# Softmax sums of a graph layer: one VectorE instruction for the leaky score, odd blocks finished on ScalarE and GpSimd

## What is computed

```python
Wh = h @ W.T
s1 = Wh @ a1
s2 = Wh @ a2
e = jax.nn.leaky_relu(s1[rows] + s2[cols], negative_slope=NEG_SLOPE)   # 0.2
e = e - jnp.max(e)
exp_e = jnp.exp(e)
sum_exp = jax.ops.segment_sum(exp_e, rows, num_segments=N)
alpha = exp_e / (sum_exp[rows] + EPS)
h_prime = jax.ops.segment_sum(alpha[:, None] * Wh[cols], rows, num_segments=N)
```

## Time and profile before

| | us |
|---|---|
| median of 3 runs | 8971.87 (8968.87 to 8975.18) |
| profiled execution | 8960.56 |
| its span in the trace | 8958.4 |
| `soft_sums`, passes 0, 1, 2 (first to last VectorE instruction of the blocks) | 236.65, 223.35, 224.63 |
| between pass 0's last and pass 1's first | 9.9 |

### The profile page before, as it was taken

The page is one execution under the profiler, slowest core; times in us unless marked ns, Lnnn a source line. Parts: engine busy times, 40 slices in busy tenths (PEclk is TensorE's granted clock), DMA queues, the critical chain, the costliest instruction groups (busy, mean ns, idle before and its releaser), DMA issues. The chain is left out here.

```text
span 8958.4 us, 195643 instructions
## 1 busy us (share of the span) xinstructions
PE 7343.9 (82%) x51013; PEld 5653.7 (63%) x51014; DVE 6057.0 (68%) x12581; ACT 5103.3 (57%) x9231; POOL 3338.0 (37%) x3274
## 2 busy tenths in 40 slices
PE   5999999888869999999877777777787877777774
PEld 3656666577758778788756556555565655555554
DVE  7988988899952222222456666666666777777777
ACT  3666666688846666666544444444456655555553
POOL 0000000000000000000067777777756777777776
PEclk8999999999989999999978888888889998988897
DMA  3333333366633333333222222222226666666665
GB/s 112 138 134 136 137 137 138 144 227 225 224 101 123 124 125 125 123 124 125 69 70 55 54 55 54 54 54 54 54 54 192 202 195 195 196 194 197 196 194 157
DMA packets 629188, 1179.08 MB, mean 132 GB/s; under 512 B 215307, under 2 KB 289340, under 8 KB 609685
## 3 DMA queue, kind: packets, MB, share of 16 engines
q1 hardware_dynamic: 499834, 860.28, 29.7%
q0 software_dynamic: 129280, 317.93, 12.7%
HBM read 901.19 MB, written 276.57 MB: 131 GB/s over the span
## 5 line engine op out<-in xcount | busy, mean ns | idle before, releaser
L2269 POOL DMA_INDIRECT att_kv_rows<-kv_dram,att_stage x1616 | 1646.1, 1019 | 520.4 <-issue 482.4
L2024 POOL DMA_INDIRECT conv_rows<-y_dram,conv_stage x1616 | 1626.9, 1007 | 501.1 <-issue 478.8
L1013 DVE SCALAR_TENSOR_TENSOR mean_rest<-mean_counts,mean_high 128x896 f16<-128x896 f32 x343 | 377.5, 1101 | 1110.5 <-ACT mean_high L974 1110.5
L694 PE MATMUL conv_part<-conv_msgs,conv_hot 128*128 128x256 f32 x3232 | 945.3, 446 | 0.0
L694 PE MATMUL att_part<-att_msgs,att_hot 128*128 128x128 f32 x3232 | 517.4, 309 | 474.1 <-DVE att_msgs L2413 434.7
L2002 ACT ACTIVATE conv_hid<-conv_hid_ps 100x512 f32<-100x512 f32 x408 | 221.0, 594 | 1179.1 <-PE conv_hid_ps L2033 1179.1
L694 PEld LDWEIGHTS conv_part<-conv_msgs,conv_hot 128*128 128x128 f32 x3232 | 710.7, 231 | 107.0
L694 PEld LDWEIGHTS att_part<-att_msgs,att_hot 128*128 128x128 f32 x3232 | 436.9, 210 | 535.7 <-issue 338.7
L1067 PE MATMUL mean_sum_ps<-wh,mean_turned 128*128 128x129 f32 x4802 | 696.2, 285 | 51.6 <-ACT mean_turned L982 51.3
L234 PE MATMUL count_ps<-count_cols,count_rows 128*128 128x392 bf16 x3920 | 730.1, 331 | 8.5 <-DVE count_cols L200 8.5
L1958 POOL MEMSET acc<- 128x6656 f32 x1 | 5.6, 5644 | 1902.8 <-POOLq L1882 1902.8
(11 more groups left out here) (279 smaller groups left out, 16592.8 us busy)
## 6 DMA issues: line engine op xcount, KB each, us to landing
c_dram<-count_counts SPq DMA_DIRECT2D x392, 392.0 KB, 2.3
mean_counts<-c_dram SPq DMA_DIRECT2D x343, 448.0 KB, 4.0
att_w_rows<-w_dram SPq DMA_DIRECT2D x404, 256.0 KB
soft_counts<-c_dram SPq DMA_DIRECT2D x98, 1024.0 KB, 4.9
w_dram<-mlp_w SPq DMA_DIRECT2D x294, 256.0 KB, 2.7
mlp_feats<-in_feats SPq DMA_DIRECT2D x295, 192.0 KB, 2.7
soft_counts<-c_dram SPq DMA_DIRECT2D x49, 1088.0 KB, 5.0
att_lanes<-lo_dram SPq DMA_DIRECT2D x404, 128.0 KB
```

The source lines that it names most:

```text
L694: ins = nc.tensor.matmul(part, c.hot[:, s, t, :], rows[:, t, :], start=half == 0 and t == 0, stop=half == 1 and t == T - 1)
L1013: nc.vector.scalar_tensor_tensor(rest[:, m], counts[:, m], 0.25, high[:, m], ALU.mult, ALU.subtract).then_inc(rest_done, 1)
L2024: pool.indirect_dma_start(rows[:, s, t, :], None, y_dram, bass.IndirectOffsetOnAxis(ap=stage[:, s, t:t + 1], axis=0)).then_inc(gathered[s] ...
L2269: pool.indirect_dma_start(kv_rows[:, s, t, :], None, kv_dram, bass.IndirectOffsetOnAxis(ap=stage[:, s, t:t + 1], axis=0)).then_inc(gathere ...
```

## The change

VectorE now makes the leaky score itself, in one scalar_tensor_tensor: max(s1 + 0.8 s2, 0.2 s1), which is the leaky score less 0.2 s2 (`bend`). `s1_low` (0.2 s1, made once for each pass) lies in the last part of `acc`; 0.8 s2 and the rest of the shift are columns of `shift`. Even blocks go on with one exponential on ScalarE and min and counts on VectorE (`weigh`). For odd blocks ScalarE takes a relu of the negated exponent, which is the min with 1, and then the exponential, and GpSimd multiplies with the counts. `weights` has six buffers instead of two, all steps work in place in them, and `exps` is gone. The loop bodies hold twelve blocks (`rounds` is 4), and VectorE and ScalarE work ahead: two blocks for even ones, five for odd ones.

```diff
-    rounds = (NW - 1) // 6
+    rounds = (NW - 1) // 12
+    evens, odds = (NW + 1) // 2, NW // 2
...
+        s1_low = acc[:, firsts[2]:NW + 1].rearrange("p n f -> p (n f)")
-        exps = sb("exps", [P, 2, 2, widest])
-        weights = sb("weights", [P, 2, widest])
-        shift = sb("shift", [P, 2, NW])
+        weights = sb("weights", [P, 6, widest])
+        shift = sb("shift", [P, 3, NW])
...
+                    elif r % 2:
+                        sp.wait_ge(weighed_even, even(p, i, r - 3))
+                    else:
+                        sp.wait_ge(weighed_odd, odd(p, i, r - 3))
...
+            @block.gpsimd
+            def _(pool):
+                for p in range(3):
+                    with pool.Fori(0, rounds) as i:
+                        for r in range(1, 12, 2):
+                            pool.wait_ge(exp_odd, odd(p, i, r))
+                            wait_counts(pool, p, i, r)
+                            nc.gpsimd.tensor_tensor(slot(p, r), slot(p, r), counts_of(p, r), ALU.mult).then_inc(weighed_odd, 1)
...
-                    dve.wait_ge(exp_done, n + 1)
-
-                    dve.wait_ge(summed, n + 1)
-                    nc.vector.tensor_tensor(here, exps[:, b, 0, 0:wide], exps[:, b, 1, 0:wide], ALU.max).then_inc(larger, 1)
-                    dve.wait_ge(counts_in[s], 16 * count)
-                    dve.wait_ge(larger, 2 + n + 1)
-                    nc.vector.scalar_tensor_tensor(here, here, 1.0, counts[:, s, 0:wide], ALU.min, ALU.mult).then_inc(weighed, 1)
+                    dve.wait_ge(summed, NW * p + w + 1)
+                    nc.vector.scalar_tensor_tensor(slot(p, r), s1_row[:, 0:wide], shift[:, 2, bass.ds(w, 1)], s1_low[:, 0:wide],
+                                                   ALU.add, ALU.max).then_inc(bent_odd if r % 2 else bent_even, 1)
+
+                def weigh(p, i, r):
+                    dve.wait_ge(exp_even, even(p, i, r))
+                    wait_counts(dve, p, i, r)
+                    nc.vector.scalar_tensor_tensor(slot(p, r), slot(p, r), 1.0, counts_of(p, r), ALU.min, ALU.mult).then_inc(weighed_even, 1)
...
+                    dve.wait_ge(s1_in[p], 16)
+                    nc.vector.tensor_scalar(s1_low[:, 0:wide], s1_row[:, 0:wide], 0.2, None, ALU.mult).then_inc(low_done, 1)
+                    dve.wait_ge(low_done, p + 1)
...
+                def body(p, i, last):
+                    for r in range(0, 12, 2):
+                        bend(p, i, r + 2)
+                        weigh(p, i, r)
+                        if not last or r < 8:
+                            bend(p, i, r + 5)
...
-                    nc.scalar.activation(exps[:, b, 0, 0:wide], row, ACT.Exp, bias=shift[:, 0, at])
-                    nc.scalar.activation(exps[:, b, 1, 0:wide], row, ACT.Exp, scale=0.2, bias=shift[:, 1, at]).then_inc(exp_done, 1)
+                    nc.scalar.activation(slot(p, r), slot(p, r), ACT.Exp, bias=shift[:, 0, bass.ds(12 * i + r, 1)]).then_inc(exp_even, 1)
+
+                def exp_of_odd(p, i, r):
+
+                    act.wait_ge(bent_odd, odd(p, i, r))
+                    nc.scalar.activation(slot(p, r), slot(p, r), ACT.Relu, scale=-1.0, bias=shift[:, 1, bass.ds(12 * i + r, 1)]).then_inc(turned, 1)
+                    act.wait_ge(turned, odd(p, i, r))
+                    nc.scalar.activation(slot(p, r), slot(p, r), ACT.Exp, scale=-1.0).then_inc(exp_odd, 1)
```

More of the change, by code:

```diff
@@ L428, in place, with slot, even, odd @@
             return ps[:, b // 3, b % 3 * (D + 1):(b % 3 + 1) * (D + 1)]
+        def slot(p, r):
+            return weights[:, (p + r) % 6, 0:widths[p] * P]
+        def even(p, i, r):
+            return evens * p + 6 * i + r // 2 + 1
+        def odd(p, i, r):
+            return odds * p + 6 * i + r // 2 + 1
         with nc.Block() as block:
@@ L442, in _ @@
                     if p > 0:
[L444 removed]
+                        sp.wait_ge(bent_even, evens * p)
+                        sp.wait_ge(bent_odd, odds * p)
                     sp.dma_start(s1_row[:, 0:wide], s1_dram[firsts[p] * P:firsts[p] * P + wide].partition_broadcast(P)).then_inc(s1_in[p], 16)
[L446 to L448 removed]
@@ L449, in _, with wait_counts, counts_of @@
-                    load(p, NW - 1, NW * p + NW - 1, p % 3)
+                    for r in range(12):
+                        load(p, 0, r, True)
+                    with sp.Fori(1, rounds) as i:
+                        for r in range(12):
+                            load(p, i, r, False)
+                    load(p, rounds, 0, False)
+            def wait_counts(eng, p, i, r):
+                eng.wait_ge(counts_in[(p + r) % 3], 16 * (4 * i + (NW * p + r) // 3 + 1))
+            def counts_of(p, r):
+                return counts[:, (p + r) % 3, 0:widths[p] * P]
@@ L477, in take @@
                     dve.wait_ge(taken, 2 * (p + 1))
[L479 to L482, removed]
-                for p in range(3):
[L484 to L491, removed]
+                def body(p, i, last):
[4 more added lines that the diff above has]
+                            bend(p, i, r + 5)
+                nc.vector.tensor_scalar(shift[:, 0], s_nodes[:, :, 1], 0.2, top[:, 2:3], ALU.mult, ALU.add).then_inc(shifts_done, 1)
+                nc.vector.tensor_scalar(shift[:, 2], s_nodes[:, :, 1], 0.8, None, ALU.mult).then_inc(shifts_done, 1)
+                dve.wait_ge(shifts_done, 2)
+                nc.vector.tensor_scalar(shift[:, 1], shift[:, 0], -1.0, None, ALU.mult).then_inc(shifts_done, 1)
+                for p in range(3):
+                    begin(p)
+                    for r in (1, 3, 0):
+                        bend(p, 0, r)
+                    with dve.Fori(0, rounds - 1) as i:
+                        body(p, i, False)
+                    body(p, rounds - 1, True)
+                    weigh(p, rounds, 0)
                     take(p)
@@ L505, in _, with exp_of_even @@
-                for p in range(3):
[L506 to L511, removed]
+                def exp_of_even(p, i, r):
+                    act.wait_ge(bent_even, even(p, i, r))
+                    nc.scalar.activation(slot(p, r), slot(p, r), ACT.Exp, bias=shift[:, 0, bass.ds(12 * i + r, 1)]).then_inc(exp_even, 1)
@@ new lines, in exp_of_odd, with body @@
+                def exp_of_odd(p, i, r):
[3 more added lines that the diff above has]
+                    nc.scalar.activation(slot(p, r), slot(p, r), ACT.Exp, scale=-1.0).then_inc(exp_odd, 1)
+                def body(p, i, last):
+                    for r in range(0, 12, 2):
+                        exp_of_even(p, i, r + 2)
+                        if not last or r < 8:
+                            exp_of_odd(p, i, r + 5)
@@ L513, in _, with sums @@
+                act.wait_ge(shifts_done, 3)
+                for p in range(3):
+                    exp_of_odd(p, 0, 1)
+                    exp_of_odd(p, 0, 3)
+                    exp_of_even(p, 0, 0)
+                    with act.Fori(0, rounds - 1) as i:
+                        body(p, i, False)
+                    body(p, rounds - 1, True)
             @block.tensor
             def _(pe):
-                def sums(p, w, n, b):
-                    pe.wait_ge(weighed, 3 + n + 1)
+                def sums(p, i, r):
+                    if r % 2:
+                        pe.wait_ge(weighed_odd, odd(p, i, r))
+                    else:
+                        pe.wait_ge(weighed_even, even(p, i, r))
```

47 lines of the change are left out of this document (26 added, 21 removed).

## The result

The changed kernel takes 9126.46 us (median of 4 runs, 9121.36 to 9128.92), the kernel before beside it 8973.08 us (8968.87 to 8975.18). The ratio is 1.0169 with a 95% interval of 1.0155 to 1.0183: 153 us slower. The profiled execution took 9128.92 us with a span of 9127.1; against the profiled one of before that is 168.7 us more of span. The prediction said 9140 us and 9105 to 9215.

What follows compares the result with a forecast made beforehand. VectorE was taken to bound the softmax passes. Steady work 158 - 3.8 + 2.8 + 6 + 5 = +168 us on the profiled 8960.56 gave 9128.6, or 9140 us on the median's footing, range 9105 to 9215.

Steps and rivals of the forecast that it cites:

- The bound, and the exclusion: Softmax passes: VectorE sets the end; its and GpSimd's two-SBUF-tensor instructions exclude each other, so their times add up; together +158 us.
- no exclusion: Softmax passes: the two engines don't exclude each other at this size, TensorE is the bound at 574 us; 8881 us, chance 0.06.
- partial exclusion: Softmax passes: half a GpSimd instruction lies beside VectorE's, a pair of blocks takes 9.1 us; about 8980 us, chance 0.06.
- the third: Softmax stage: the shared time isn't kept full, +20 us; with code loads and clock 9226 us or more, chance 0.08.
- What a GpSimd instruction adds: Each odd block's multiplication adds 4.43 us at 2048 columns, 4.71 us at 2176; bounds 4.2 and 4.75 us.
- GpSimd's code: MODIFY_POOL_CONFIG inside pass 0's loop delays GpSimd: nothing up to 39 us, +5 us taken.
- The end of a pass: Last two weighings of each pass stand in a row, TensorE ends 1.5 us or more later: 2 a pass, +6 us.
- Start and s1_low: Pass 0 begins about 1787.9 instead of 1791.68, -3.8 us; the extra tensor_scalar in passes 1 and 2 costs +2.8 us.
- The loads: Counts' loads in the passes: chain of 23 to 25 us for six blocks that take 33.9, so hidden.
- TensorE: In the passes it needs 7.66 of 11.3 us a pair, idle 3.6; lower clock is covered, +0 taken, up to 10 us.
- the second one: Sign of being wrong: in a pass VectorE stands idle for TensorE or the counts.

Runs made afterwards that it cites:

- the relu version: Against the kernel before: no GpSimd, VectorE makes relu(s1 + s2) in one one-input tensor_scalar, the target node's factor cancels; ratio 0.9868, once more 0.9894.

## Why the prediction was right, point by point

**The bound, and the exclusion.** Right. The sum of both engines' times gave the passes within 1% in pass 0 and 2% in the others: 291.7, 275.5 and 275.5 us forecast, 289.9, 269.7 and 269.6 measured. The four runs that moved one thing each (no GpSimd, half of it, almost none, another operand) went as exclusion wants, and the rivals "no exclusion" and "partial exclusion" fall. So does the third, for the shared time was kept full: 0.6 or 0.7 us of passes 1 and 2 are used by neither engine. The trace of before had told it in stages that the change doesn't touch.

**What a GpSimd instruction adds.** 4.43 us forecast at 2048 columns. A waiting one ended 4.41 us after VectorE's. The sum charged too much elsewhere: I kept VectorE's price at 2.286 us, the kernel before's, in which small waits are contained; 222.01 / 98 = 2.265 is what its instruction costs in the new order. The one behind GpSimd costs 2.15, since its start lies under the other's end. 2 x 2.265 + 2.15 + 4.41 = 11.09 us a pair, and two pairs took 22.03 (from 2131.45 to the same place at 2153.48). The sum was too high by 5.8 us in pass 1 and 5.9 in pass 2, 0.24 us a pair, and by about as much in pass 0 once the code's 4 us there are counted apart (see "GpSimd's code"): some 17.5 us in all. With the code the passes grew by 144.5 us, not by 158 + 5.

**The end of a pass.** Here the step failed by size: +6 us forecast, +16.7 measured. VectorE's copies wait 11.15, 9.37 and 8.22 us for TensorE where they waited 12.0 in all before. I had counted two late blocks. In pass 0 there are three:

```profile
2067.00 6.25 POOL L494 TENSOR_TENSOR soft_weights<-soft_weights,soft_counts 128x2176 f32<-128x2176 f32 x1 [0.70 <-DMA soft_counts<-c_dram]
2068.50 9.35 DVE L508 SCALAR_TENSOR_TENSOR soft_weights<-soft_weights,soft_counts 128x2176 f32<-128x2176 f32 x2
...
2075.67 13.29 PE L586 MATMUL soft_ps<-wh,soft_weights 128*128 x102 [3.16 <-DVE soft_weights L508]
2089.00 2.17 DVE L522 COPY acc<-soft_ps 128x1935 f32<-128x1935 f32 x1 [11.15 <-PE soft_ps L586]
```

The last multiplication holds up the weighing of block 46, so 46, 47 and 48 come free together and TensorE does 102 matmuls after it had stood idle. A queue that is fed by two engines ends later by what both deliver last.

**GpSimd's code.** +5 us taken, about 4 found. The eight MODIFY_POOL_CONFIG (two in each turn of pass 0's loop) are there, and pass 0 has 4.5 us in which neither engine works, VectorE's opening wait for ScalarE. GpSimd could have used it: the first odd block's exponential was ready at 1796.03. But the first MODIFY_POOL_CONFIG stands there, at 1796.26, and the first multiplication starts 6.8 us later. In the changed kernel with the counts loaded once it stands at 1779.9, ahead of the wait, and the first multiplication follows the exponential at once:

```profile
1803.07 6.23 POOL L494 TENSOR_TENSOR soft_weights<-soft_weights,soft_counts 128x2176 f32<-128x2176 f32 x1 [23.95 <-issue]
```

```profile
L484 POOLq MODIFY_POOL_CONFIG  x8: 1/6/11, 1779.9 to 1995.8; - x8
1795.88 13.14 POOL L484 TENSOR_TENSOR soft_weights<-soft_weights,soft_counts 128x2176 f32<-128x2176 f32 x2 [17.00 <-ACT soft_weights L551]
```

Its pass 0 has no time that neither engine uses, and is 4.9 us shorter where the others are 1 us shorter. The later turns cost nothing that shows: in the run with the bend from PSUM and the counts loaded once, the multiplication follows 2.3 to 2.6 us after each of them.

**Start and s1_low.** As said: the first bend at 1788.0 instead of 1791.68, the tensor_scalar 1.22 us in the others.

**The loads.** "Hidden" was right for the changed kernel, with less margin than I worked out. The run with the bend from PSUM shows the buffers binding at 9.3 us a pair, so their chain takes some 28 us for six blocks, not 23 to 25, where the changed kernel takes 33.

**TensorE.** Its idle time in pass 1 is 59 us in eleven pieces, one for every two pairs, so 2.4 us a pair, not 3.6; at the lower clock its matmuls take more of the pass (194.94 us for 185.48). The 574 us that the first rival gave it were too high as well: in the steady stream of the relu version its three passes take 544.

**The sign of being wrong.** Taken by its words, the second one came up: VectorE stands idle in pass 1 for 33.7 us for TensorE and 3.2 for the counts. The sign was badly chosen. All but 0.7 us of that lies inside GpSimd's instructions, when VectorE could not have run, so it says nothing against the sum.

**The sum.** 144.5 (the code's 4 us in it) - 3.7 + 2.5 + 16.7 = 160.0 us, and in the traces the last copy of the stage moves from 2499.70 to 2659.73, by 160.0. The two profiled executions differ by 168.7, as forecast, but 8.7 of that lies in later stages that the change doesn't touch: the first gather stage alone takes 10 us more in this trace. The medians differ by 153. So +168 was right for the pair of profiles partly by luck. In the stage it was 8 us too high, as the rest of two errors of +17.5 and -10.7 and a small one at the code, and the later stages happened to add 8.7. The 153 us of the medians lie inside the stated range all the same.

## What to carry to other kernels

Before work is moved from VectorE to GpSimd, look for a place in the trace where both are busy and compare the durations with those of the same line alone. If they exclude each other, the moved instruction costs GpSimd's time, not zero: here 4.4 us to save 2.3. What helped was fewer input tensors for each element: a factor that cancels later turned one of the two instructions of two inputs into one of one input, and that was worth 118 to 139 us. The six slots and the work ahead came with it; in the changed kernel's order they were worth 0 to 3 us a pass.

A long "idle until DMA" of an engine isn't a cost by itself; the same loads cost 1 us a pass under one bound and 42 under the next.

## What was new about the hardware

- The order of turns is kept strictly: a waiting GpSimd instruction is served between two queued ones of VectorE (2122.17, 2123.38 and 2124.81 in the timeline above, and 70 of 72 times in the stage), which no row of before showed.
- A PSUM operand takes a two-tensor instruction of VectorE out of the exclusion: at most 2.484 us beside GpSimd, against 7.043 with both in SBUF. The Trainium skill ("SBUF — State Buffer", section "Who interferes with whom") lets a VectorE instruction with at most one SBUF input run beside GpSimd outside its two-port modes; the trace agrees for PSUM as the second source.
- A tensor_scalar of one SBUF input, which takes 1.22 us for 2048 columns where the two-tensor forms take 2.28, is held as well: 5.54 us. The same section of the Trainium skill names tensor_scalar among the instructions that can enter a two-port mode and then take the shared ports. The run agrees in that the instruction is held; which mode it ran in, no trace here shows.
- TensorE's granted clock, at the higher level (2.4 GHz) for nearly all of a pass before (0.98), fell to 0.84 or 0.85 in the passes, a mixture of both levels. Before, TensorE had 47 waits of 0.7 us in pass 1, and now it has 11 of 5.4 us. Inside the passes that cost nothing, since TensorE still had 59 us over. At the end of pass 0 it does add to the time: 102 matmuls take 13.29 us at 0.87, where three such blocks take 11.6 in the steady stream of the relu version.
- MODIFY_POOL_CONFIG delays the first instruction behind it: 6.8 us in the changed kernel (1796.26 to 1803.07). A repeated one in the same loop delayed it by no more than 2.3 to 2.6 us.
- The first of the two gather stages takes 2117 and 2127 us in the two profiles on one chip (first to last matmul) and 2570 to 2640 on others, while the passes of the changed kernel repeat to 0.1 us on two chips and those of the relu version to 1.3 us. A change in the softmax stage is better read from its passes than from the total.
